# Causal attention layer with a sixth buffer of probabilities, its rotation tables loaded span by span

## The chip, the cores and the metric

The kernel runs on 1 core of one Trainium2 chip. The metric is the device time of one execution in microseconds (us), the median of several runs.

## The reference

One transformer layer in float32 on x of 4 batches, 2048 positions and 256 features, with 16 heads of 16. Attention with rotated queries and keys, then a block that projects onto cosines and sines of learned angles:

```python
qkv = layernorm(x) @ w_qkv                       # 256 -> 3 x 256
Q, K = Q * cos + rotate_half(Q) * sin, K * cos + rotate_half(K) * sin
attn = softmax(causal(Q @ K.T * 16 ** -0.5))     # per batch and head, 2048 x 2048
x = x + (attn @ V) @ w_proj + b_proj
real = layernorm(x) @ cos(theta + theta_noise)
imag = layernorm(x) @ sin(phi + phi_noise)
x = x + sqrt(real * real + imag * imag)
```

## The kernel before, in words

The work is cut into 16 units (u), each one batch and four heads, and each unit into four spans (c or t) of 512 positions, which makes 64 spans. A span has SUB (t + 1) steps of 128 keys against its 512 queries, 640 steps in all.

For each span (u, c), in this order:
- TensorE projects queries and keys (L1012), ScalarE copies them out as `raw` (L1158), SyncE's queue moves halves of it into `rot` (L742). GpSimd turns them (`rope`, L664 to L682: `raw` by `cos_t`, `rot` by `sin_t`, their sum, then three bf16 parts). SyncE lays the parts into `queries` and `stack_k` (L758). For the first two spans VectorE does the turning (L1360), and for the first five TensorE projects the swapped halves too (L1024).
- A first pass finds each query's maximum: TensorE multiplies queries by keys (L1057, items "max"), VectorE reduces the banks (L1399, L1394). GpSimd splits the negative maximum into three parts (L1510 and on), TensorE turns it (L1065, "turn"), VectorE copies it as `max_t` (L1351), SyncE lays it as three more rows of `queries` (L768).
- A second pass makes scores less the maximum (L1079), a step having four products of 512 columns, one a head, fewer columns on the diagonal. ScalarE takes the exponent (L1198) into `probs`, GpSimd zeroes the corner of diagonal tiles (L1526), and TensorE sums the values (L1094) into one bank that the whole span shares. ScalarE copies that bank out (L1205, "lift").
- Where four units of a batch are through, the rest of the layer runs for its blocks (L946, L935, L1001 and others).

Scores have four banks of the eight, the other work shares banks 2 to 6 with them, and the values' sum has the last. `probs` is a ring of `PROBS` buffers, one a step. Before it overwrites the buffer of step g, ScalarE waits until the values of step g - PROBS are summed:

```python
if g >= PROBS and n == 0:
    act.wait_ge(s_av, g - PROBS + 1)
```

Every engine follows a list, `ORDER[engine]`, in program order and waits on semaphores. The lists come from `plan()`, which runs before the kernel is built: every job has an engine, a duration, an aim in units of the whole (`at`), predecessors and a lag; engine by engine the job is taken that has the earliest aim among those that can start soon. The leads (`MAX_LEAD`, `QK_LEAD`, `EARLY`, `V_LEAD`, `X_LEAD`), `PATIENCE`, `SLACK`, `HOLD`, `RUN` and `STICK` are numbers of this planner and in no instruction. `TURN_COST` is its charge for a move between the values' products and all others, since the values' products stand side by side in the array (17 columns each, four at a time).

Names: `emptied` and `filled` are waits on a bank's reader and on its writer. `s_rope` counts seven operations of rotation a span. `PLACE[u, c]` is i, the number of a span in the order in which spans are projected.

Of the kernel before, what the change touches and what calls it, by code (L numbers as in the profile page):

```python
# [14 lines left out]
P = 128  # L15
BATCH, SEQ, DIM, HEADS = 4, 2048, 256, 16
# [5 lines left out]
KT = DIM // P  # L22
SPAN = 512
# [42 lines left out]
PROBS = 5  # L66
# [12 lines left out]
URGENT = .526  # L79
# [78 lines left out]
MAX_LEAD = .578  # L158
QK_LEAD = .737

EARLY = .545
X_LEAD = .189
V_LEAD = .418
SLACK = .9
PATIENCE = .008
# [5 lines left out]
TURN_COST = .1  # L171
MAX_FIRST = .033
HOLD = .763
STICK = 0
RUN = 4.358
TURN_LAG = .725
MAX_SLACK = .02
# [16 lines left out]
PACE = .924  # L194
LAST_AT = 15.4
LAST_PULL = .181
# [10 lines left out]
def plan():  # L207
# [41 lines left out]
    for c in range(1, SPANS):  # L249
        job(("tables", c), "SP", 0.9, CLOCK[0, c - 1] - 1.05, [("qk", 0, c - 1, KT - 1)], 5.0)  # L250
# [8 lines left out]
    for at, kind, u, c in sorted(todo):  # L259
# [12 lines left out]
        elif kind == "qk":  # L272
# [7 lines left out]
            free = [("rope", *last, ROPE_OPS - 1), *([("tables", c)] if c and u == 0 else [])] if i < ROPE_DVE else [used]  # L280
# [8 lines left out]
            for n in range(2 if i < ROPE_DVE else 0, ROPE_OPS):  # L289
                after = [("out", ("qk", u, c, 1)), ("rope", u, c, n - 1), ("rope", *last, ROPE_OPS - 1)]  # L290
                after += [("rot", u, c), ("out", ("qr", u, c))] if n in (1, 2) else []
                after += [("fetch", *ago), ("fetch_k", *ago)] if n == 3 else []
                after += [("tables", c)] if n == 0 and c and u == 0 else []
                if i < ROPE_DVE:
                    job(("rope", u, c, n), "DVE", 0.44 if n in (3, 5) else 0.69, at, after, 0.03 if n < ROPE_OPS - 1 else None)
                else:
                    job(("rope", u, c, n), "POOL", 0.7 if n in (3, 5) else 1.28, at, after)
# [191 lines left out]
def layer_kernel(nc, x, w_qk, w_v, w_proj, b_proj, theta, phi, theta_noise, phi_noise, cosines, sines,  # L489
# [7 lines left out]
    with ExitStack() as ctx:  # L497
# [44 lines left out]
        cos_t = sb("cos_t", [P, SEQ])  # L542
        sin_t = sb("sin_t", [P, SEQ])
# [49 lines left out]
        s_tables = [sem(f"rotation_tables_loaded{n}") for n in range(SPANS)]  # L593
# [58 lines left out]
        def rope(engine, ops, u, c, n):  # L652
            i = PLACE[u, c]
            span = slice(c * SPAN, (c + 1) * SPAN)
# [5 lines left out]
            if n == 0:  # L660
                emptied(engine, ("qk", u, c, 1))
                if i < FIRST * SPANS:
                    engine.wait_ge(s_tables[c], 32)
                ins = ops.tensor_tensor(turned[:, :], raw[:, i % 2, :], cos_t[:, span], ALU.mult)  # L664
            elif n == 1:
# [4 lines left out]
                ins = ops.tensor_tensor(crossed[:, :], rot[:, i % 2, :], sin_t[:, span], ALU.mult)  # L670
# [52 lines left out]
        with nc.Block() as block:  # L723
            @block.sync
            def _(sp):
# [142 lines left out]
                for name in ORDER["SP"]:  # L868
# [3 lines left out]
                    elif kind == "tables":  # L872
                        load_tables(name[1])
# [272 lines left out]
            def _(act):  # L1146
# [95 lines left out]
                act.dma_start(cos_t[:, 0:SPAN], cosines[:, 0:SPAN]).then_inc(s_tables[0], 16)  # L1242
                act.dma_start(sin_t[:, 0:SPAN], sines[:, 0:SPAN]).then_inc(s_tables[0], 16)
# [23 lines left out]
            def _(dve):  # L1267
# [75 lines left out]
                def reduce_out(item):  # L1343
# [9 lines left out]
                    if item[0] in ("qk", "qr"):  # L1353
                        u, c = item[1:3]
                        i, span = PLACE[u, c], slice(c * SPAN, (c + 1) * SPAN)
                        dve.wait_ge(s_tables[c], 32)
                        if i:
                            dve.wait_ge(s_rope, ROPE_OPS * i)
                        to, table = (turned, cos_t) if item[0] == "qk" else (crossed, sin_t)
                        nc.vector.tensor_tensor(to[:, :], bank, table[:, span], ALU.mult).then_inc(s_emptied["DVE"], 1)  # L1360
# [197 lines left out]
def tables():  # L1558
# [12 lines left out]
    return lay(cos), lay(sin), np.eye(P, dtype=np.float32), corner, one  # L1571
# [27 lines left out]
```

## Time and profile before

| | before |
|---|---|
| median of 3 runs | 1975.45 us (1974.7 to 1977.72) |
| profiled execution, its own time | 1979.04 us |
| span of its instructions | 1977.3 us |
| TensorE busy | 1939.0 us, 98% |
| VectorE / ScalarE / GpSimd busy | 1559.9 / 1389.1 / 871.0 us |
| bytes moved by DMA | 133.30 MB, 67 GB/s |
| matmul records | 12036 |

The span runs from the first to the last instruction of the profiled execution, and its own time has some 1.7 us around that. A matmul of float32 has several records. Matmuls overlap in their pipeline, so the distance between two starts tells what one costs, and a record's length does not.

### The profile page before, as it was taken

How to read it: one execution, taken by the hardware profiler on the slowest of the kernel's cores; microseconds unless marked ns; L12 is line 12 of the kernel's file. 1: busy time of each engine (PE TensorE's matmuls, PEld its weight loads, DVE VectorE, ACT ScalarE, POOL GpSimd, SP SyncE). 2: the span in 40 equal slices, each digit the busy share in tenths (PEclk: the TensorE clock that was granted, in tenths of full speed). 3: DMA queues.
4: the chain of work that ended last, by engine and by line, in shares of the span. 5: the costliest groups of instructions: out<-in, count | busy, mean ns of one | idle time of the engine just before them, and what ended most of it. 6: DMA issues, size and time to landing. Idle time of an engine off the chain costs nothing.

```text
span 1977.3 us, 38203 instructions
## 1 busy us (share of the span) xinstructions
PE 1939.0 (98%) x12036; PEld 798.1 (40%) x12036; DVE 1559.9 (79%) x4101; ACT 1389.1 (70%) x2687; POOL 871.0 (44%) x1336
## 2 busy tenths in 40 slices
PE   7999999999999999999999999999999999999998
PEld 4333433334443434343443443434444344433335
DVE  5898789988778787887877878888777877879725
ACT  3466668877676777877767777777767767777883
POOL 4714615443535454633544435553444545431232
PEclk9999999999999999999999999999999999999999
DMA  6301312122121221311222121322212212120131
GB/s 143 97 24 28 121 47 73 39 71 65 52 73 54 74 83 64 105 35 64 61 71 77 57 72 56 104 68 71 72 33 71 68 64 78 51 94 7 49 105 57
DMA packets 130762, 133.30 MB, mean 67 GB/s; under 512 B 29434, under 2 KB 105722, under 8 KB 130554
## 3 DMA queue, kind: packets, MB, share of 16 engines
q1 hardware_dynamic: 127728, 128.29, 21.1%
q10 hardware_dynamic: 2832, 2.56, 0.7%
q8 instruction: 97, 1.59, 0.3%
q14 instruction: 105, 0.86, 0.2%
HBM read 38.49 MB, written 25.68 MB: 32 GB/s over the span
## 4 chain that ended last, share of the span: by engine, by line
PE 87%; ACT 5%; issue 2%; DVE 2%; DMA 2%; POOL 1%; SPq 0%; DVEq 0%; POOLq 0%; ACTq 0%
PE banks L1094 23%; PE banks L1079 23%; PE banks L1057 22%; PE banks L1012 6%; PE banks L1001 6%; ACT probs L1198 3%; PE banks L1039 3%; PE banks L946 2%; DVE chunk_max L1399 1%; PE banks L935 1%; DMA squares<-sums 1%; PE banks L928 1%; PE banks L1065 0%; DVE banks L1394 0%; PE banks L1024 0%
## 5 line engine op out<-in xcount | busy, mean ns | idle before, releaser
L1198 ACT ACTIVATE probs<-banks 128x512 f32<-128x512 f32 (+1 forms) x2240 | 1143.9, 602 | 328.6 <-PE banks L1079 289.3
L1399 DVE TENSOR_REDUCE chunk_max<-banks 128x1 f32<-128x512 f32 x1536 | 985.3, 683 | 216.7 <-PE banks L1057 215.0
L1079 PE MATMUL banks<-queries,stack_k 99*128 99x512 bf16 (+3 forms) x2560 | 740.5, 350 | 11.8 <-ACT probs L1198 4.1
L1057 PE MATMUL banks<-stack_k,queries 96*128 96x512 bf16 (+3 forms) x2560 | 712.2, 349 | 8.2 <-DMA queries<-parts 2.8
L1394 DVE CUSTOM_DVE_ANT_0 banks<-banks,row_mask 128x128 f32<-128x128 f32 (+3 forms) x1024 | 483.7, 508 | 87.4 <-PE banks L1057 86.8
L1094 PE MATMUL banks<-probs,v_one 128*17 128x512 f32 (+3 forms) x5120 | 527.8, 532 | 1.1 <-POOL probs L1526 0.6
L1079 PEld LDWEIGHTS banks<-queries,stack_k 99*128 99x128 bf16 x2560 | 231.4, 97 | 435.9 <-ACT probs L1198 218.7
L1057 PEld LDWEIGHTS banks<-stack_k,queries 96*128 96x128 bf16 x2560 | 233.0, 97 | 310.9 <-DVE chunk_max L1399 67.3
L1526 POOL TENSOR_SCALAR_AFFINE_SELECT probs<-probs 128x512 f32<-128x512 f32 x256 | 160.9, 638 | 402.5 <-ACT probs L1198 402.0
L1094 PEld LDWEIGHTS banks<-probs,v_one 128*17 128x17 f32 x5120 | 119.7, 96 | 266.3 <-issue 173.7
L1394 DVE DVE_READ_ACCUMULATOR2_ANT chunk_max<- 128x1 f32 x1024 | 144.0, 141 | 0.0
L664 POOL TENSOR_TENSOR turned<-raw,cos_t 128x512 f32<-128x512 f32 x62 | 78.7, 1270 | 136.9 <-ACT raw L1158 135.4
L1012 PE MATMUL banks<-x_t,wqk 128*128 128x512 f32 x256 | 123.7, 606 | 0.7 <-ACT x_t L1153 0.5
L670 POOL TENSOR_TENSOR crossed<-rot,sin_t 128x512 f32<-128x512 f32 x62 | 80.8, 1304 | 61.3 <-DMA rot<-raw 58.3
L1510 POOL TENSOR_SCALAR max_neg<-row_max 128x16 f32<-128x16 f32 x64 | 19.2, 300 | 183.6 <-DVE row_max L1408 143.6
L1001 PE MATMUL banks<-wave,heads_t 128*128 128x512 f32 x208 | 98.7, 597 | 0.0
L1158 ACT ACTIVATE raw<-banks 128x512 f32<-128x512 f32 x62 | 37.4, 603 | 74.0 <-PE banks L1012 74.0
L672 POOL TENSOR_TENSOR turned<-turned,crossed 128x512 f32<-128x512 f32 x62 | 80.5, 1298 | 4.2
L1498 POOL TENSOR_TENSOR inverse<-squares 128x512 f32<-128x512 f32 x24 | 30.4, 1268 | 109.6 <-ACT squares L1177 109.6
L678 POOL TENSOR_TENSOR crossed<-turned,parts 128x512 f32<-128x512 f32 x62 | 71.8, 1158 | 4.6
L682 POOL TENSOR_TENSOR parts<-crossed,parts 128x512 bf16<-128x512 f32 x62 | 71.7, 1157 | 4.4
L1177 ACT ACTIVATE squares<-banks 128x512 f32<-128x512 f32 x52 | 31.1, 598 | 54.5 <-PE banks L1001 54.5
(158 smaller groups left out, 1162.3 us busy)
## 6 DMA issues: line engine op xcount, KB each, us to landing
queries<-parts SPq DMA_DIRECT2D x384, 64.0 KB, 2.6
stack_k<-parts SPq DMA_DIRECT2D x354, 64.0 KB, 2.6
sums<-o_raw SPq DMA_DIRECT2D x64, 256.0 KB, 2.3
rot<-raw SPq DMA_DIRECT2D x236, 64.0 KB, 2.0
xin<-x SPq DMA_DIRECT2D x17, 512.0 KB, 4.2
mid<-x SPq DMA_DIRECT2D x13, 512.0 KB, 5.1
heads_t<-sums SPq DMA_DIRECT2D x26, 256.0 KB
inverse<-inverses SPq DMA_DIRECT2D x26, 256.0 KB
```

The costliest lines, as they stand in the source:

```text
L664: ins = ops.tensor_tensor(turned[:, :], raw[:, i % 2, :], cos_t[:, span], ALU.mult)
L670: ins = ops.tensor_tensor(crossed[:, :], rot[:, i % 2, :], sin_t[:, span], ALU.mult)
L672: ins = ops.tensor_tensor(turned[:, :], turned[:, :], crossed[:, :], ALU.add)
L1001: mm = nc.tensor.matmul(bank, turned3[finish_set(n)][:, k, j * P:(j + 1) * P], wave[:, k, :], start=(k == 0), stop=(k == KT - 1))
L1012: mm = nc.tensor.matmul(psum[BANK[item]], wqk[:, u % GROUPS, k, :], x_t[:, k, c * SPAN:(c + 1) * SPAN], start=(k == 0), stop=(k == KT - 1) ...
L1057: mm = nc.tensor.matmul(bank[:, n * wide:(n + 1) * wide], queries[0:SPLIT_ROWS, query_place(u, t), h + n, j * P:(j + 1) * P], stack_k[u % ...
L1079: mm = nc.tensor.matmul(bank[:, a * wide:(a + 1) * wide], stack_k[u % 2][0:ROWS, j // SUB, first + a, (j % SUB) * P:(j % SUB + 1) * P], qu ...
L1094: mm = nc.tensor.matmul(out_bank[VW * h:VW * h + VC, w0:SPAN], v_one[u // 2 % 2][:, j, HG * (u % 2) + h, :], probs[:, g % PROBS, h, w0:SPA ...
L1198: nc.scalar.activation(probs[:, g % PROBS, first:first + many, w0:SPAN], bank, ACT.Exp).then_inc(s_exp, 1)
L1394: ins = nc.vector.tensor_tensor_reduce(out=scores_of, in0=scores_of, in1=row_mask[:, SPAN - wide:SPAN], scale=1.0, scalar=LOWEST, op0=ALU. ...
L1399: nc.vector.tensor_reduce(to, bank[:, 0:count * wide].rearrange("p (h n) -> p h n", h=count), AX.X, ALU.max).then_inc(s_emptied["DVE"], 1)
L1526: nc.gpsimd.affine_select(out=square, in_=square, compare_op=ALU.is_ge, fill=0.0, base=0, pattern=[[0, HG], [1, P]], channel_multiplier=-1 ...
```

## The change

Three things. The tables `cos_t` and `sin_t`, 8 KB each in every partition and loaded once, go. In their place stands `turn_t`, two buffers of 4 KB that hold cosines and sines of one span. It is loaded for each of the 64 spans with one DMA of 512 KB (ScalarE's queue has the first, SyncE's the other 63), and a load waits until the span two before has read its buffer. The 8 KB that come free are a sixth buffer of `probs`. And the planner's numbers are others, among them those below, so all lists are made anew (`SLACK` .9 to 1.3, `PATIENCE` .008 to .012, `HOLD` .763 to .542, `RUN` 4.358 to 4.842, `STICK` 0 to .001, `V_LEAD` .418 to .325, `PACE` .924 to .989 besides).

```diff
-PROBS = 5
+PROBS = 6
...
-MAX_LEAD = .578
-QK_LEAD = .737
-EARLY = .545
+MAX_LEAD = 0.63
+QK_LEAD = 0.718
+EARLY = 0.691
...
-    for c in range(1, SPANS):
-        job(("tables", c), "SP", 0.9, CLOCK[0, c - 1] - 1.05, [("qk", 0, c - 1, KT - 1)], 5.0)
...
+            if i:
+                job(("tables", u, c), "SP", 0.6, at - 0.1, [("qk", *last, KT - 1), *([used] if i > 1 else [])], 4.0)
+            free = [("rope", *last, ROPE_OPS - 1), ("tables", u, c)] if i < ROPE_DVE else [used]
...
-                after += [("tables", c)] if n == 0 and c and u == 0 else []
+                after += [("tables", u, c)] if n == 0 else []
...
-        cos_t = sb("cos_t", [P, SEQ])
-        sin_t = sb("sin_t", [P, SEQ])
+        turn_t = sb("turn_t", [P, 2, 2, SPAN])
...
             if n == 0:
                 emptied(engine, ("qk", u, c, 1))
-                if i < FIRST * SPANS:
-                    engine.wait_ge(s_tables[c], 32)
-                ins = ops.tensor_tensor(turned[:, :], raw[:, i % 2, :], cos_t[:, span], ALU.mult)
+                engine.wait_ge(s_tables[i % 2], 16 * (i // 2 + 1))
+                ins = ops.tensor_tensor(turned[:, :], raw[:, i % 2, :], turn_t[:, i % 2, 0, :], ALU.mult)
...
-                ins = ops.tensor_tensor(crossed[:, :], rot[:, i % 2, :], sin_t[:, span], ALU.mult)
+                ins = ops.tensor_tensor(crossed[:, :], rot[:, i % 2, :], turn_t[:, i % 2, 1, :], ALU.mult)
...
-                def load_tables(c):
-                    columns = slice(c * SPAN, (c + 1) * SPAN)
-                    sp.dma_start(cos_t[:, columns], cosines[:, columns]).then_inc(s_tables[c], 16)
-                    sp.dma_start(sin_t[:, columns], sines[:, columns]).then_inc(s_tables[c], 16)
+                def load_tables(u, c):
+                    i = PLACE[u, c]
+                    if i - 2 in range(ROPE_DVE):
+                        emptied(sp, ("qr", *PROJECTED[i - 2]))
+                    elif i >= 2:
+                        sp.wait_ge(s_rope, ROPE_OPS * (i - 2) + 2)
+                    sp.dma_start(turn_t[:, i % 2, :, :], rotations[:, c, :, :]).then_inc(s_tables[i % 2], 16)
...
-                act.dma_start(cos_t[:, 0:SPAN], cosines[:, 0:SPAN]).then_inc(s_tables[0], 16)
-                act.dma_start(sin_t[:, 0:SPAN], sines[:, 0:SPAN]).then_inc(s_tables[0], 16)
+                act.dma_start(turn_t[:, 0, :, :], rotations[:, 0, :, :]).then_inc(s_tables[0], 16)
...
-    return lay(cos), lay(sin), np.eye(P, dtype=np.float32), corner, one
+    return np.stack([lay(cos), lay(sin)], 1).reshape(P, 2, SPANS, SPAN).transpose(0, 2, 1, 3), np.eye(P, dtype=np.float32), corner, one
```

In the lists below the lines of the changed kernel are mostly one higher (L1095 is L1094). All instructions of computation are the same in kind and number, but for one filler product.

TensorE, unit 2, its first span of four diagonal steps (the values of 512, 384, 256 and 128 columns). Before, from the second of these steps to the third; L1057 is a product for a maximum, L1079 one for scores:

```order
L1094 MATMUL banks<-probs,v_one 17x384 x4
L1057 MATMUL banks<-stack_k,queries 128x512 x2
L1057 MATMUL banks<-stack_k,queries 128x128 x4
L1079 MATMUL banks<-queries,stack_k 128x128 x4
L1057 MATMUL banks<-stack_k,queries 128x512
L1079 MATMUL banks<-queries,stack_k 128x512
L1057 MATMUL banks<-stack_k,queries 128x512 x2
L1079 MATMUL banks<-queries,stack_k 128x512 x2
L1057 MATMUL banks<-stack_k,queries 128x512
L1079 MATMUL banks<-queries,stack_k 128x512
L1094 MATMUL banks<-probs,v_one 17x256 x4
```

The changed kernel, from the end of the same span's scores on:

```order
L1058 MATMUL banks<-stack_k,queries 128x512
L1058 MATMUL banks<-stack_k,queries 128x256 x2
L1095 MATMUL banks<-probs,v_one 17x512 x4
L1095 MATMUL banks<-probs,v_one 17x384 x4
L1095 MATMUL banks<-probs,v_one 17x256 x4
L1095 MATMUL banks<-probs,v_one 17x128 x4
L1080 MATMUL banks<-queries,stack_k 128x512 x2
L1058 MATMUL banks<-stack_k,queries 128x512 x2
```

The four steps of values, which stood in four places, now stand in one.

TensorE, the start: from the turn of the first span's maxima (L1065) to its first scores. Before:

```order
L1065 MATMUL banks<-ident_bf,max_parts 48x128
L1057 MATMUL banks<-stack_k,queries 128x512 x2
L1057 MATMUL banks<-stack_k,queries 128x128 x4
L1057 MATMUL banks<-stack_k,queries 128x512 x2
L1057 MATMUL banks<-stack_k,queries 128x256 x2
L1057 MATMUL banks<-stack_k,queries 128x512 x2
L1039 MATMUL banks<-wv,x_t 128x128 x8
L1057 MATMUL banks<-stack_k,queries 128x256 x2
L1057 MATMUL banks<-stack_k,queries 128x512
L1057 MATMUL banks<-stack_k,queries 128x384
L1079 MATMUL banks<-queries,stack_k 128x512
```

The changed kernel (L1066, L1058 and L1080 are the same lines):

```order
L1066 MATMUL banks<-ident_bf,max_parts 48x128
L1058 MATMUL banks<-stack_k,queries 128x512 x2
L1058 MATMUL banks<-stack_k,queries 128x128 x4
L1058 MATMUL banks<-stack_k,queries 128x512 x2
L1058 MATMUL banks<-stack_k,queries 128x256 x2
L1058 MATMUL banks<-stack_k,queries 128x512 x2
L1058 MATMUL banks<-stack_k,queries 128x256 x2
L1058 MATMUL banks<-stack_k,queries 128x512
L1058 MATMUL banks<-stack_k,queries 128x384
L1080 MATMUL banks<-queries,stack_k 128x512 x2
```

The projection of values (L1039) has left this stretch, and the first scores come two at a time. It stands now behind the projections of unit 1's first two spans.

SyncE's queue, about a third of the way, where a block's last part is under way. Before:

```order
L742 DMA rot<-raw 32x512 x4
L768 DMA queries<-max_t 1x16x128 x3
L848 DMA mid<-x 128x4x256
L774 DMA sums<-o_raw 128x512
L768 DMA queries<-max_t 1x16x128 x3
L742 DMA rot<-raw 32x512 x4
L758 DMA queries<-parts 16x4x512 x6
L758 DMA stack_k<-parts 16x4x512 x6
L768 DMA queries<-max_t 1x16x128 x3
```

The changed kernel, the same stretch:

```order
L735 DMA turn_t<-rotations 128x1024
L743 DMA rot<-raw 32x512 x4
L775 DMA sums<-o_raw 128x512
L769 DMA queries<-max_t 1x16x128 x3
L735 DMA turn_t<-rotations 128x1024
L743 DMA rot<-raw 32x512 x4
L735 DMA turn_t<-rotations 128x1024
L743 DMA rot<-raw 32x512 x4
L769 DMA queries<-max_t 1x16x128 x3
```

A table load stands ahead of each move of halves. All through the program 34 of SyncE's 63 loads have such a move directly behind them, and six have the rows of a maximum (L769).

## Rows read from the trace of the kernel before

**Rows 1.** The page, parts 1 and 2: engines, and the granted TensorE clock in 40 slices.

```profile
PE 1939.0 (98%) x12036; PEld 798.1 (40%) x12036; DVE 1559.9 (79%) x4101; ACT 1389.1 (70%) x2687; POOL 871.0 (44%) x1336
...
PEclk9999999999999999999999999999999999999999
```

**Rows 2.** The page, part 4: the chain that ended last, by engine and by line.

```profile
PE 87%; ACT 5%; issue 2%; DVE 2%; DMA 2%; POOL 1%; SPq 0%; DVEq 0%; POOLq 0%; ACTq 0%
PE banks L1094 23%; PE banks L1079 23%; PE banks L1057 22%; PE banks L1012 6%; PE banks L1001 6%; ACT probs L1198 3%; PE banks L1039 3%; PE banks L946 2%; DVE chunk_max L1399 1%; PE banks L935 1%; DMA squares<-sums 1%; PE banks L928 1%; PE banks L1065 0%; DVE banks L1394 0%; PE banks L1024 0%
```

**Rows 3.** Windows of all engines: busy us (instructions), clock, DMA share, GB/s.

```profile
0.00:100.00 100.00, 83.76 (x462) 38.72 (x463) 70.50 (x206) 37.22 (x68) 60.44 (x103) 0.97 0.50 119
...
1300.00:1700.00 400.00, 398.90 (x2491) 164.72 (x2489) 318.97 (x832) 288.76 (x561) 188.39 (x260) 1.00 0.22 66
...
1884.00:1896.00 12.00, 11.95 (x76) 2.74 (x68) 1.78 (x2) 12.00 (x27) 3.31 (x2) 1.00 0.27 94
```

**Rows 4.** Waits: engine, line, releaser: us in total, times, longest.

```profile
ACT probs L1198 <- PE banks L1079: 289.3, 220, 3.6
PEld banks L1079 <- ACT probs L1198: 218.7, 609, 1.0
...
ACT probs L1198 <- PE banks L1094: 29.4, 23, 2.2
```

**Rows 5.** Timeline of TensorE at 403 us: start, us, instructions.

```profile
402.96 0.38 PE L1057 MATMUL banks<-stack_k,queries 96*128 96x512 bf16 x1
403.18 0.38 PE L1079 MATMUL banks<-queries,stack_k 99*128 99x512 bf16 x1
403.40 0.38 PE L1057 MATMUL banks<-stack_k,queries 96*128 96x512 bf16 x1
403.62 0.38 PE L1079 MATMUL banks<-queries,stack_k 99*128 99x512 bf16 x1
403.93 1.91 PE L1094 MATMUL banks<-probs,v_one 128*17 128x512 f32 x16
405.77 0.39 PE L1079 MATMUL banks<-queries,stack_k 99*128 99x512 bf16 x1
```

**Rows 6.** Timeline of TensorE in the last unit, where no maxima are left, 1885 us.

```profile
1884.51 1.04 PE L1079 MATMUL banks<-queries,stack_k 99*128 99x512 bf16 x4
1885.48 1.05 PE L1094 MATMUL banks<-probs,v_one 128*17 128x512 f32 x8
1886.46 1.05 PE L1079 MATMUL banks<-queries,stack_k 99*128 99x512 bf16 x4
```

**Rows 7.** Timeline of all engines around the first scores.

```profile
44.46 0.24 PE L1065 MATMUL banks<-ident_bf,max_parts 128*48 128x128 bf16 x1
...
46.06 1.86 SPq L768 DMA_DIRECT2D queries<-max_t  x3
...
48.77 2.02 PE L1039 MATMUL banks<-wv,x_t 128*128 128x128 f32 x16 [0.35 <-DVE chunk_max L1399]
...
51.96 0.38 PE L1079 MATMUL banks<-queries,stack_k 99*128 99x512 bf16 x1 [0.57 <-DMA queries<-max_t]
```

**Rows 8.** Timeline of the start: a table load, and the rotation that reads it.

```profile
24.44 1.58 SPq L733 DMA_DIRECT2D cos_t<-cosines  x1
...
34.83 1.28 POOL L664 TENSOR_TENSOR turned<-raw,cos_t 128x512 f32<-128x512 f32 x1 [4.28 <-ACT raw L1158]
```

**Rows 9.** Tile cos_t, then tile max_t: duration min/median/max; landings min/median/max.

```profile
L733 SPq DMA_DIRECT2D cos_t<-cosines x3: 506/611/1577, 12.9 to 30.0; - x3
...
DMA to landing us min/median/max: 4.0/5.1/6.1
...
L768 SPq DMA_DIRECT2D queries<-max_t x192: 502/589/1623, 46.1 to 1879.4; - x192
...
DMA to landing us min/median/max: 1.6/1.7/4.5
```

**Rows 10.** The page, part 3: the hardware DMA queue of SyncE.

```profile
q1 hardware_dynamic: 127728, 128.29, 21.1%
```

More of the change, by code:

```diff
@@ L78 @@
 ROPE_DVE = 2
-URGENT = .526
+URGENT = 0.526
 HELP = 5
@@ L157 @@
 MASKED_HEADS = 4
-MAX_LEAD = .578
-QK_LEAD = .737
-EARLY = .545
[L162 to L165, printed above, removed]
+MAX_LEAD = 0.63
+QK_LEAD = 0.718
+EARLY = 0.691
+X_LEAD = 0.187
+V_LEAD = 0.325
+SLACK = 1.3
+PATIENCE = 0.012
 TRIG_AT = 2.0
@@ L170 @@
 OTHER_BANKS = range(2, 7)
[L171 to L177, printed above, removed]
+TURN_COST = 0.1
+MAX_FIRST = 0.036
+HOLD = 0.542
+STICK = 0.001
+RUN = 4.842
+TURN_LAG = 0.76
+MAX_SLACK = 0.02
 FINISHED = [SPANS * b + t for b in range(BATCH) for u, t in SCORED if u == GROUPS * b + GROUPS - 1]
@@ L192 @@
 IN_HALVES = range(BLOCKS - SPANS, BLOCKS)
-PACE = .924
+PACE = 0.989
 LAST_AT = 15.4
-LAST_PULL = .181
+LAST_PULL = 0.181
 SETS = SPANS
@@ L279, in plan @@
                 before_qk = ("qk", u, c, k)
-            free = [("rope", *last, ROPE_OPS - 1), *([("tables", c)] if c and u == 0 else [])] if i < ROPE_DVE else [used]
+            if i:
+                job(("tables", u, c), "SP", 0.6, at - 0.1, [("qk", *last, KT - 1), *([used] if i > 1 else [])], 4.0)
+            free = [("rope", *last, ROPE_OPS - 1), ("tables", u, c)] if i < ROPE_DVE else [used]
             reader, took = ("DVE", 0.69) if i < ROPE_DVE else ("ACT", 0.6 if i < HELP else 0.5)
@@ L486, with layer_kernel @@
     NUMBER |= {item: n for n, item in enumerate(name for name in ORDER["PE"] if READER.get(name) == _e)}
-def layer_kernel(nc, x, w_qk, w_v, w_proj, b_proj, theta, phi, theta_noise, phi_noise, cosines, sines,
+def layer_kernel(nc, x, w_qk, w_v, w_proj, b_proj, theta, phi, theta_noise, phi_noise, rotations,
                  identity, corner, ones, w_last, sums, inverses, out):
@@ L592, in layer_kernel @@
         s_wv = sem("value_weights_loaded")
-        s_tables = [sem(f"rotation_tables_loaded{n}") for n in range(SPANS)]
+        s_tables = [sem(f"rotation_tables_loaded{n}") for n in range(2)]
         s_corner = sem("diagonal_mask_loaded")
@@ L653, in rope @@
             i = PLACE[u, c]
-            span = slice(c * SPAN, (c + 1) * SPAN)
             if i < ROPE_DVE and n == 2:
@@ L872, in _ @@
                     elif kind == "tables":
-                        load_tables(name[1])
+                        load_tables(*name[1:])
                     elif kind == "wv":
@@ L1354, in reduce_out @@
                         u, c = item[1:3]
-                        i, span = PLACE[u, c], slice(c * SPAN, (c + 1) * SPAN)
-                        dve.wait_ge(s_tables[c], 32)
+                        i = PLACE[u, c]
+                        dve.wait_ge(s_tables[i % 2], 16 * (i // 2 + 1))
                         if i:
                             dve.wait_ge(s_rope, ROPE_OPS * i)
-                        to, table = (turned, cos_t) if item[0] == "qk" else (crossed, sin_t)
-                        nc.vector.tensor_tensor(to[:, :], bank, table[:, span], ALU.mult).then_inc(s_emptied["DVE"], 1)
+                        to, table = (turned, 0) if item[0] == "qk" else (crossed, 1)
+                        nc.vector.tensor_tensor(to[:, :], bank, turn_t[:, i % 2, table, :], ALU.mult).then_inc(s_emptied["DVE"], 1)
                         return
@@ L1577 @@
     from concourse.bass_utils import run_bass_kernel_spmd
-    cosines, sines, eye, corner, one = tables()
+    rotations, eye, corner, one = tables()
     w = np.asarray(L0_attn_w_qkv)
@@ L1587 @@
         "theta": L0_ffn_theta, "phi": L0_ffn_phi, "theta_noise": L0_ffn_theta_noise, "phi_noise": L0_ffn_phi_noise,
-        "cosines": cosines, "sines": sines, "eye": eye, "corner": corner, "one": one,
+        "rotations": rotations, "eye": eye, "corner": corner, "one": one,
         "w_last": w_last.reshape(P, DIM),
```

## The prediction

> **What bounds the kernel now.** I read the page from the top: engines first, then the chain, then the windows, the waits, and last the timeline of TensorE.
>
> TensorE is busy 98% of the span, at full clock in every slice [rows 1], and the chain that ended last lies on it for 87%, with ScalarE 5%, VectorE 2% and DMA 2% [rows 2]. All the products remain, so the change can only save time between them. The windows say where such time is: in the first 100 us TensorE is busy 83.76, from 1300 to 1700 us 398.90 of 400 [rows 3]. The page's busy time flatters it, though, since matmuls overlap. The distance between two starts is the honest measure, and rows 5 show it: products of 512 columns start 0.22 us apart, so each sets its own pace, but before the values' products (L1094) the distance is 0.31.
>
> So there are two kinds of lost time. One is the move between the values' products, of 17 columns side by side, and the rest, of 128 columns. Going in costs 0.31 - 0.22 = 0.09 us. For the way out: one step of values takes 0.98 us to the next start [rows 6], two steps take 1.84 [rows 5], so a step is 0.86 and what is left over is 0.12, some of it rounding. I take 0.10 us a change. The other kind is waiting for a bank: the weight loads of scores stand idle 218.7 us for ScalarE in 609 waits, short ones that the pipeline mostly covers [rows 4]. On the chain the exponents (L1198) hold 3%, 59 us, and the maxima's reduction (L1399) 1% [rows 2]. ScalarE in turn waits 289.3 us for scores and only 29.4 us, in 23 waits, for values [rows 4]. The latter holds what five buffers of `probs` cost, together with the bank of the values' sum, for which the same row stands. So the ring is rarely the limit by itself. What a sixth buffer buys is freedom for the order: values may wait longer and go in fewer, longer stretches.
>
> **Changes between kinds of product.** I counted them in the two lists of TensorE. The values stand in 302 stretches before and in 281 now, 21 fewer, thus 42 changes fewer. The turns of maxima, of 48 columns, are a kind of their own: 27 of their edges touched a stretch of values, now 15, which costs 12 changes back. In all 715 become 685, and 30 x 0.10 = 3.0 us is saved. TensorE pays them itself, one behind the other, so this is on the path except where ScalarE is the limit. It is that in the last unit, busy 12.00 of 12 us [rows 3]; there the change is free and saves nothing, but few of the 30 lie there.
>
> A page of the Trainium skill bears on this price: TensorEngine Tiling (Array Packing), section Key Properties, says that changing the tiling mode, not just the tile, drains the TensorE. By that rule longer stretches are always better. The trace agrees at 0.09 us on the way in; against it stands that a longer stretch keeps scores from ScalarE, which the rule does not price.
>
> **Waits at the banks.** No row prices one stretch's waits. The lower bound is nothing: the same exponents follow the same scores. The upper is the chain's 59 us on L1198 shared among 302 stretches, 0.20 us each, for 21 stretches 4.1 us. I take the upper one, as the sixth buffer loosens the 23 waits for values besides, and keep 0 for the range. Beyond it, half of the 29.4 us, 14.7, is the most that I can imagine from a ring that no longer binds; it is a rival below.
>
> **The start.** Between the turn of the first maxima at 44.46 us and the first scores at 51.96 lie 7.5 us [rows 7]. The order has only some 3.4 us of products there, at rows 5's pace; the rest is waiting for VectorE and, at the end, 0.57 us for the three DMAs of rows [rows 7]. In this hole the projection of values (2.02 us, 48.77) cost next to nothing. It is moved out, and must be paid later in full if TensorE has no hole there: between 0 and 2.0 us lost, I take 1.0. Scores that come two at a time win a little of it back.
>
> **Table loads.** SyncE issues 63 loads in place of six DMAs, ScalarE one in place of two. An issue takes 0.61 us at the median and lands 5.1 us later (4.0 to 6.1) for 256 KB [rows 9]; these are of 512 KB. That is 63 x 0.61 = 38 us of issue on a queue that has the whole span for it, less 4 us. The bytes: 64 loads of 0.52 MB less 2.1 MB for the old tables are 31.5 MB more, on 128.29 MB that held 21.1% of the engines [rows 10], so some 5% more, in bursts. A load's own wait, on the second rotation step of the span two before, is the one that the move of halves already had. Where the load stands directly ahead of that move (34 places), GpSimd starts the rotation not with `raw` but up to 6 us later. It is cover that pays: in the order the maxima that need a span begin 60 us or more of products behind its projection, in both kernels, from unit 1 on. Only unit 0 is tight, with 8 to 42 us. Its third span's table was issued at 24.44 us and read at 34.83 [rows 8]; now its issue waits for the same queue place, and 24.44 + 1.58 + 6.1 = 32.1 is still before 34.83. With that cover gone, each late microsecond would be one of the start. I set the loads at 0.
>
> **The rest.** The leads of the maxima grow (`MAX_LEAD`). From turn to first scores of a span the order has at least 10.8 us of products before and 17.7 now, from unit 1 on, against 7.5 that the transfer needed at its slowest [rows 7]: late rows become less likely, which cost little already. The price stands at the end, where 92 products of scores are left behind the last maximum instead of 87, in the stretch that ScalarE limits: five times the difference of an exponent (some 0.49 us, 12.00 us over some 24.5) and a product (0.22), 1.4 us at most, and the finish products lie between. I set 0.
>
> **Sum.** -3.0 - 4.1 + 1.0 = -6.1 us. Against the profiled execution's own 1979.04 that is 1972.9. It lies 3.6 us above the median of the three runs, 1975.45, so for the median the sum gives 1969.3 us. A measurement of this kernel can tell about 0.2%, 4 us, from no change.
>
> **Rivals.**
> (a) Only the counted changes come: the waits at the banks move elsewhere, since ScalarE's work is the same and a stretch of three full values steps, 0.86 x 3 = 2.6 us, outlasts four full banks of 0.6. Stretches of three full steps' columns or more grow from 47 to 53. Then -3.0 + 1.0 = -2.0, 1973.5 us. For it: VectorE is at 80% and ScalarE at 72% from 1300 to 1700 us, where TensorE hardly waits [rows 3]; there is little to win there. Chance 0.27.
> (b) The ring was the limit: 14.7 us of ScalarE's waits for values come back, -3.0 - 14.7 + 1.0, 1958.8 us. Against it: 23 waits of 640 steps [rows 4]. Chance 0.13.
> (c) Slower: rows of a maximum land behind a table in unit 0. The DMAs are busy half of the first 100 us [rows 3], rows landed after 1.7 us at the median and after 4.5 at worst [rows 9], and the order, counted at the pace of rows 5, leaves 2.5, 4.4, 5.6 and 9.0 us of products between turn and scores in the four spans of unit 0. If three of them wait the table's 6.1 us less the 1.7, 3 x 4.4 = 13.2, the sum is -6.1 + 13.2 = +7.1, 1982.5 us. It decides from two late spans on. Against it: behind unit 0 the lead is 17.7 us, and TensorE has VectorE to wait for at the start anyway. Chance 0.12.
> The Trainium skill, DMA: Bandwidth & Descriptors, section Queues, rings and completion order, says that a DMA's semaphore lands only after every earlier write of the same DMA engine, across queues. By that rule (c) would strike wherever rows follow a table within some 6 us; no row here shows the two together.
> (d) That the sixth buffer isn't used: the order excludes it, since the values of 54 steps stand behind scores five or six steps ahead, and before those of 25.
>
> **How the numbers follow.** The forecast, 1969.3, has 0.48, the rivals 0.27, 0.13 and 0.12. The range reaches from just above (b), as its full price is an extreme, to a little over the end of (a) with 2.0 lost at the start and a late span: 1959.5 to 1978.5. Faster by over 0.2% is below 1971.5: all of (b) and most of the forecast's 0.48, in which the waits may give only part, and a little of (a), 0.61 together. Slower is above 1979.4: 0.11 of (c) and 0.01 for the rest, 0.12. Within lies 0.27.
>
> **What would show it.** Right: TensorE's busy time nearly the same and the span shorter by 4 to 9 us; ScalarE's waits for values below 29.4 us in 23; the chain's share on L1198 a little below 3%; turn_t landing in 4 to 8 us, and GpSimd waiting for it ahead of a rotation with nobody waiting behind. Wrong: the first 100 us busier or emptier by more than 2 us than 83.76, TensorE waiting for `queries<-max_t` or `queries<-parts` after unit 0, or ScalarE's waits for scores above 289.3 us with the chain's ScalarE share above 5%, which would be starvation by the longer stretches.

## The result and the profile after

The changed kernel took 1984.77 us (median of 5 runs, 1977.54 to 1990.46) against 1976.64 for the kernel before on the same chip: ratio 1.0042, interval 1.0024 to 1.0061. It is slower, by about 8 us, where the prediction's sum was 6.1 us of gain, its forecast 1969.3 us and the top of its range 1978.5. A second series, of 12 runs, gave 1984.2 us and 1.0032 (1.0019 to 1.0046), so the sign stands.

The page of the changed kernel: TensorE's row, the granted clock in 40 slices, SyncE's queue, and the two lines on the chain that ended last.

```profile
PE 1948.0 (98%) x12034; PEld 805.0 (40%) x12034; DVE 1559.4 (78%) x4101; ACT 1388.9 (70%) x2687; POOL 870.5 (44%) x1336
...
PEclk9989999899999999999999999999999999999999
...
q1 hardware_dynamic: 135936, 159.75, 26.5%
...
PE 85%; ACT 4%; DMA 3%; SPq 3%; issue 2%; DVE 1%; POOL 1%; ACTq 0%; DVEq 0%; POOLq 0%
PE banks L1080 23%; PE banks L1095 22%; PE banks L1058 22%; PE banks L1002 5%; PE banks L1013 5%; PE banks L1040 3%; ACT probs L1199 3%; PE banks L947 2%; SPq L759 1%; DMA rot<-raw 1%; SPq L743 1%; PE banks L936 1%; PE banks L929 1%; PE banks L1066 1%; DMA xin<-x 0%
```

Against [rows 1, 2] three things are to be seen. TensorE's share is still 98%, but its clock is below 90% in two slices, the third (99 to 149 us) and the eighth (348 to 398 us). The chain now holds SyncE's queue with 3% and DMAs with 3%, among them the move of halves (`rot<-raw`), which stood nowhere in it. And the queue moves 159.75 MB for 128.29 [rows 10], as computed.

Where did the time go? The share of busy time cannot say, since TensorE's busy time grows when its clock falls. I took the distances between the starts of its products, as the prediction did at rows 5, over the whole profiled execution, and split them into three: the pace of the products themselves, 0.097 us for each change of kind (fitted over the traces; the prediction's rows gave 0.09 on the way in and 0.12 on the way out), and what is left, which is waiting and lost clock. The first two are a fit, so their split from the third is an estimate.

| us, TensorE from first to last product | before | after | difference |
|---|---|---|---|
| the products' own pace | 1809.1 | 1808.5 | -0.6 |
| changes of kind | 69.4 (715) | 66.4 (685) | -3.0 |
| lost | 86.3 | 102.1 | +15.8 |
| of it 0 to 100 us | 21.3 | 23.3 | +2.0 |
| of it 100 to 200 us | 5.4 | 12.5 | +7.1 |
| of it 200 to 500 us | 10.1 | 21.1 | +11.0 |
| of it 500 to 1900 us | 39.6 | 34.3 | -5.3 |
| of it the rest | 6.3 | 7.6 | +1.3 |

(The parts count waits of at least 20 ns, so they add up to a little less.) The sum, +12.2, stands for the two profiled executions, 1979.04 and 1990.46 us; the medians differ by 8.1. The changed kernel's profiled execution was the slowest of its five. So in this pair a gain like the forecast one is there, in the changes and in the body of the program, and some 20 us of losses in the first 500 us eat it up. Two places hold most of them. A second profile of the same kernel (1983.11 us, near its median) has the losses from 100 to 200 us and from 300 to 400 us again, each within 1 us, but not the one in the first 100 us: there it lost less than the kernel before. And at 1337 us it has no wait of that length.

**Place A, 341 to 372 us.** Timeline of the changed kernel, all engines (start, duration, instructions, idle time before with what ended it):

```profile
340.87 1.06 SPq L775 DMA_DIRECT2D sums<-o_raw  x2
...
341.97 0.45 SPq L735 DMA_DIRECT2D turn_t<-rotations  x1
342.46 1.20 SPq L727 DMA_DIRECT2D xin<-x  x2
...
343.71 0.50 SPq L735 DMA_DIRECT2D turn_t<-rotations  x1
344.31 2.67 SPq L743 DMA_DIRECT2D rot<-raw  x4
...
346.66 1.28 POOL L662 TENSOR_TENSOR turned<-raw,turn_t 128x512 f32<-128x512 f32 x1 [1.09 <-DMA turn_t<-rotations]
...
354.08 1.27 POOL L668 TENSOR_TENSOR crossed<-rot,turn_t 128x512 f32<-128x512 f32 x1 [6.14 <-DMA rot<-raw]
...
358.42 2.07 ACT L1212 ACTIVATE xin<-xin,shift,rstd 128x256 f32<-128x256 f32 x4 [5.40 <-POOL shift L698]
...
361.03 1.91 PE L1095 MATMUL banks<-probs,v_one 128*17 128x512 f32 x8 [3.95 <-ACT probs L1199]
```

Read it from the bottom. TensorE waits 3.95 us for exponents. ScalarE had not made them because it stood 5.40 us at the normalisation of the next block's `x` (L1212), which is ahead of them in its list. That waits for GpSimd's shift (L698), and GpSimd stood 6.14 us at the rotation's second half, for `rot<-raw`. The four transfers of `rot` were issued behind two sums, two tables and two pieces of `x`, 2.5 MB in 3.4 us. They usually land after 2.3 us. Here the last of the four, which sets GpSimd free, landed after 7.7, the longest of all 236. The rotation itself was in no hurry: its span's maxima come much later, as the prediction said. What was in a hurry stood behind it, on two engines' in-order lists.

Then comes a second price. Windows of the changed kernel (PE, PEld, DVE, ACT and POOL busy, each with its count; granted clock, DMA share, GB/s):

```profile
345.00:360.00 15.00, 11.90 (x82) 4.18 (x80) 13.28 (x50) 7.65 (x16) 7.12 (x13) 0.98 0.81 235
360.00:372.00 12.00, 10.97 (x45) 2.72 (x46) 4.79 (x15) 7.36 (x15) 9.18 (x19) 0.60 0.10 24
```

For 15 us the DMA engines are 81% busy and TensorE is idle 3.1 us. In the next 12 us it waits one more and does 45 products only: from 359.3 us on, while it still waited, it was granted 1.2 GHz in place of 2.4, for 10.2 us. The same happens, smaller, at two more places. A product that starts at 480.07 us has waited 2.90 us, and the clock is halved for 6.8 us from 478.8 on. The one at 1337.45 has waited 2.36 us for GpSimd's `max_parts`, which stand there behind another wait for `rot<-raw`, of 3.74 us; the clock is halved for 3.4 us from 1338.9 on. The first of these, in the same kind of timeline:

```profile
478.66 1.23 DVE L1309 TENSOR_TENSOR heads_t<-heads_t,inverse 128x1024 f32<-128x1024 f32 x1 [5.43 <-DMA inverse<-inverses]
479.81 0.21 DVE L1351 COPY max_t<-banks 48x128 bf16<-48x128 bf16 x1
480.07 0.61 PE L1058 MATMUL banks<-stack_k,queries 96*128 96x512 bf16 x1 [2.90 <-DVE max_t L1351]
```

Again the late transfer (`inverse`, issued at 470.08 us) isn't what TensorE needs. It needs the small copy of 0.21 us that stands behind the transfer's reader on VectorE. That the table loads made this transfer late is argued from the run with the move first, below, and not shown in this trace.

In all the changed kernel has some 41 us at half clock, in stretches of 3.4, 6.8 and 10.2 us; the kernel before has some 10.

**Place B, 100 to 120 us.** Windows of the kernel before, then of the changed one:

```profile
100.00:110.00 10.00, 9.91 (x81) 4.84 (x80) 9.66 (x27) 5.41 (x11) 3.54 (x5) 1.00 0.15 48
110.00:120.00 10.00, 9.75 (x54) 2.67 (x52) 10.00 (x23) 6.79 (x13) 0.00 (x0) 1.00 0.18 61
```

```profile
100.00:110.00 10.00, 8.86 (x65) 2.87 (x63) 10.00 (x26) 3.89 (x8) 4.49 (x10) 1.00 0.17 57
110.00:120.00 10.00, 9.62 (x23) 2.91 (x23) 10.00 (x24) 3.30 (x6) 0.00 (x0) 0.51 0.17 58
```

VectorE is full in both. In the changed kernel TensorE has little else than maxima here, and each waits for it:

```profile
109.20 0.39 PE L1058 MATMUL banks<-stack_k,queries 96*128 96x256 bf16 x2 [0.21 <-DVE chunk_max L1399]
109.80 0.39 PE L1058 MATMUL banks<-stack_k,queries 96*128 96x512 bf16 x1 [0.21 <-DVE chunk_max L1399]
...
119.40 2.41 PE L1040 MATMUL banks<-wv,x_t 128*128 128x128 f32 x16
```

The projection of values, which filled this stretch at 107.61 us before, now stands at 119.40. From 110 us on the clock is halved for 10.2 us, and 23 products run where 54 did.

### The profile page after: what moved, and what is told of

It reads as the page before. It is cut to its first block, busy times and chain, and to the rows that moved or that the text cites. A ratio compares the mean times of both kernels' runs of the same rounds, so it can differ in the third digit from the quotient of the medians.

```text
span 1988.7 us, 38254 instructions
## 1 busy us (share of the span) xinstructions
PE 1948.0 (98%) x12034; PEld 805.0 (40%) x12034; DVE 1559.4 (78%) x4101; ACT 1388.9 (70%) x2687; POOL 870.5 (44%) x1336
## 3 DMA queue, kind: packets, MB, share of 16 engines
q1 hardware_dynamic: 135936, 159.75, 26.5%
## 4 chain that ended last, share of the span: by engine, by line
PE 85%; ACT 4%; DMA 3%; SPq 3%; issue 2%; DVE 1%; POOL 1%; ACTq 0%; DVEq 0%; POOLq 0%
PE banks L1080 23%; PE banks L1095 22%; PE banks L1058 22%; PE banks L1002 5%; PE banks L1013 5%; PE banks L1040 3%; ACT probs L1199 3%; PE banks L947 2%; SPq L759 1%; DMA rot<-raw 1%; SPq L743 1%; PE banks L936 1%; PE banks L929 1%; PE banks L1066 1%; DMA xin<-x 0%
## 5 line engine op out<-in xcount | busy, mean ns | idle before, releaser
L1199 ACT ACTIVATE probs<-banks 128x512 f32<-128x512 f32 (+1 forms) x2240 | 1139.9, 600 | 340.8 <-PE banks L1080 314.3
L1080 PE MATMUL banks<-queries,stack_k 99*128 99x512 bf16 (+3 forms) x2560 | 737.5, 351 | 5.8 <-ACT probs L1199 1.9
L1058 PE MATMUL banks<-stack_k,queries 96*128 96x512 bf16 (+3 forms) x2560 | 716.4, 351 | 12.0 <-DMA queries<-parts 2.9
L1095 PE MATMUL banks<-probs,v_one 128*17 128x512 f32 (+3 forms) x5120 | 524.3, 532 | 4.3 <-ACT probs L1199 4.3
L1080 PEld LDWEIGHTS banks<-queries,stack_k 99*128 99x128 bf16 x2560 | 234.3, 97 | 416.4 <-ACT probs L1199 219.6
L1058 PEld LDWEIGHTS banks<-stack_k,queries 96*128 96x128 bf16 x2560 | 233.9, 98 | 338.3 <-DVE chunk_max L1399 80.3
L1095 PEld LDWEIGHTS banks<-probs,v_one 128*17 128x17 f32 x5120 | 121.3, 97 | 270.1 <-issue 168.3
L668 POOL TENSOR_TENSOR crossed<-rot,turn_t 128x512 f32<-128x512 f32 x62 | 80.5, 1299 | 58.3 <-DMA rot<-raw 54.3
L662 POOL TENSOR_TENSOR turned<-raw,turn_t 128x512 f32<-128x512 f32 x62 | 78.9, 1272 | 40.4 <-issue 30.4
L1206 ACT ACTIVATE o_raw<-banks 128x512 f32<-128x512 f32 x64 | 38.6, 603 | 44.1 <-PE banks L1095 43.8
```

Source lines behind the costliest of these rows:

```text
L662: ins = ops.tensor_tensor(turned[:, :], raw[:, i % 2, :], turn_t[:, i % 2, 0, :], ALU.mult)
L668: ins = ops.tensor_tensor(crossed[:, :], rot[:, i % 2, :], turn_t[:, i % 2, 1, :], ALU.mult)
L1058: mm = nc.tensor.matmul(bank[:, n * wide:(n + 1) * wide], queries[0:SPLIT_ROWS, query_place(u, t), h + n, j * P:(j + 1) * P], stack_k[u % ...
L1080: mm = nc.tensor.matmul(bank[:, a * wide:(a + 1) * wide], stack_k[u % 2][0:ROWS, j // SUB, first + a, (j % SUB) * P:(j % SUB + 1) * P], qu ...
L1095: mm = nc.tensor.matmul(out_bank[VW * h:VW * h + VC, w0:SPAN], v_one[u // 2 % 2][:, j, HG * (u % 2) + h, :], probs[:, g % PROBS, h, w0:SPA ...
L1199: nc.scalar.activation(probs[:, g % PROBS, first:first + many, w0:SPAN], bank, ACT.Exp).then_inc(s_exp, 1)
```

## The experiments

Three questions: is it the table loads or the plan of the work; within the loads, is it their bytes or their place in the queue; and what do the sixth buffer and the numbers do apart from each other. Kernels that ran together shared a chip and its runs of the kernel before.

**Tables of almost no bytes.** The rows that are left out keep the angles of earlier spans; lists and waits are those of the changed kernel.

```diff
+rows = slice(0, P if i < 8 else 4)
-sp.dma_start(turn_t[:, i % 2, :, :], rotations[:, c, :, :])
+sp.dma_start(turn_t[rows, i % 2, :, :], rotations[rows, c, :, :])
```

> The changed kernel, whose table loads from the ninth span on carry 4 partitions instead of 128 (the other rows of the tables stay those of earlier spans, so later rotations use wrong angles): same orders, same waits, same number of issues, 29 MB less traffic. Theory T1 (the bytes of the table loads crowd other transfers, which land late, in-order engines stand behind them, and TensorE's clock then falls to half): 1966 to 1973 us, granted clock back at about 0.997, no landing of rot over 4.5 us. Theory T2 (the new orders themselves leave the waits, the bytes are harmless): 1982 to 1988 us, clock 0.989 to 0.993 as before.

1971.3 us, ratio 0.9969 (0.9957 to 0.9982). Without the bytes, the change as a whole is faster than the kernel before. Two of the signs were missed: the granted clock came back to 0.993 to 0.995 only (the stretch at half clock from 109 us on is still there), and the longest landing of `rot` was 5.1 us.

**All bytes, but another place in the queue.** Wherever a table load stood directly ahead of a move of halves (34 places), the two change places in SyncE's list. Nothing else differs.

```diff
+for _n in range(len(ORDER["SP"]) - 1):
+    _a, _b = ORDER["SP"][_n:_n + 2]
+    if _a[0] == "tables" and _b[0] == "rot":
+        ORDER["SP"][_n:_n + 2] = [_b, _a]
```

> The changed kernel with one edit of SyncE's list: wherever a table load stands directly ahead of a move of halves, the two change places, so the move no longer stands behind 512 KB. T1 with the table itself as the obstacle (T3: the place in the queue decides): most of the loss comes back, 1972 to 1978 us, median landing of rot 2.0 us again. T1 with crowding by several large transfers together: little changes, 1981 to 1987 us, since x blocks and other loads still stand ahead. T2: 1982 to 1988 us.

1973.17 us, 0.9979 (0.9970 to 0.9989). Timeline of this kernel at place A:

```profile
342.32 2.57 SPq L747 DMA_DIRECT2D rot<-raw  x4
...
344.93 0.58 SPq L739 DMA_DIRECT2D turn_t<-rotations  x1
...
349.13 1.27 POOL L672 TENSOR_TENSOR crossed<-rot,turn_t 128x512 f32<-128x512 f32 x1 [3.15 <-DMA rot<-raw]
```

And its windows:

```profile
345.00:360.00 15.00, 14.49 (x104) 4.87 (x96) 14.51 (x56) 11.13 (x22) 10.67 (x21) 1.00 0.58 170
360.00:372.00 12.00, 11.96 (x75) 4.17 (x75) 10.57 (x35) 10.46 (x21) 10.54 (x20) 1.00 0.20 58
```

The rotation runs 5 us earlier (2 of them this kernel was already ahead at its last rotation, 329.61 for 331.66 us), TensorE has no wait of over 1.5 us behind it, it does 104 and 75 products in place of 82 and 45, and the clock stays full. Over the whole profiled execution 83.3 us are lost in place of 102.1; of these 18.8 us, 16.6 lie in the three hundreds of us from 300, from 400 and from 1300 on, where the long waits stood. As many bytes, the same numbers, the same buffers: the queue place alone is worth the 10 us. VectorE's wait for `inverse` also fell, from 5.43 to 2.85 us, and TensorE's wait of 2.90 us behind it is gone.

**Half the bytes.** The rows of the first experiment with `P // 2` in place of 4.

> The changed kernel whose table loads from the ninth span on carry 64 partitions instead of 128 (the other rows stay those of earlier spans, so later rotations use wrong angles there). T1 says that the loss grows with the bytes ahead of other transfers: between 1971.3 us (4 partitions) and 1984.8 us (128), 1974 to 1980 us. If any large load ahead does the harm whatever its size: 1982 to 1988 us.

1984.63 us, 1.0030 (1.0015 to 1.0045): nothing gained. Timeline of this kernel at place A, and its windows:

```profile
351.80 1.27 POOL L668 TENSOR_TENSOR crossed<-rot,turn_t 128x512 f32<-128x512 f32 x1 [5.28 <-DMA rot<-raw]
```

```profile
345.00:360.00 15.00, 12.52 (x89) 4.22 (x87) 13.09 (x49) 9.63 (x19) 8.85 (x17) 0.97 0.64 157
360.00:372.00 12.00, 12.00 (x69) 3.99 (x65) 9.00 (x30) 9.18 (x19) 10.13 (x23) 0.89 0.11 25
```

The forecast of 1974 to 1980 us, a loss that grows with the bytes, was missed. GpSimd's wait is graded: 6.14 us with full tables, 5.28 with half, 3.37 with four rows, 3.15 with the move first. The cost isn't: at 5.28 us TensorE still waits 2.48 us in this stretch, at 3.37 and 3.15 it has no such wait. Some 3 to 5 us, by an estimate from these four, is what stood as slack between the rotation and the engines behind it. The kernel still lost 3.4 us of half clock at 359 us, and as much again at 854 and 1329.

**The ring alone taken back.** The changed kernel with five buffers.

```diff
-PROBS = 6
+PROBS = 5
```

> The changed kernel with five buffers of probabilities, planned anew with the same numbers; table loads as in the changed kernel. T1: as slow as the changed kernel, 1983 to 1990 us, clock 0.989 to 0.994. If the sixth buffer's longer stretches are the cause (part of T2): back to 1975 to 1979 us.

1998.71 us, 1.0102 (1.0082 to 1.0122), slower than either theory had it. **The ring and the tables without the numbers:** the changed code planned with the numbers of before.

> The changed kernel with the planner's numbers of the kernel before (six buffers, tables span by span). Changes between kinds of product 711, stretches of values 302, as before. T1: slow, 1980 to 1990 us, clock under 0.995, since the table loads are all there. T2 with the numbers as the cause: 1974 to 1978 us.

1987.34 us, 1.0054 (1.0038 to 1.0069). The time is the one that the theory of the bytes had forecast, but its cause is another: the clock is at 0.995 to 0.998, not under 0.995, and the run of this plan with the move first, below, gains nothing. The profiled execution took 7.4 us more than that of before, 1986.39 for 1979.04: 2.9 for more filler products (products that the plan puts where it expects TensorE to have nothing else), 4.3 for more waits (90.6 us for 86.3), and 0.4 less for changes, 711 of them. Here is where the fillers stand, in TensorE's timeline near the end, for the kernel before and for this one:

```profile
1939.69 1.95 PE L1102 MATMUL banks<-ident 128*128 128x128 f32 x16
```

```profile
1942.58 6.41 PE L1103 MATMUL banks<-ident 128*128 128x128 f32 x56
```

**Tables span by span, and nothing else:** five buffers, numbers of before.

> The kernel before with the tables loaded span by span and nothing else: five buffers, the planner's numbers of before, planned anew since the load is a job of SyncE's list. It prices the table loads alone. T1 (bytes ahead of other transfers make in-order engines wait): 1983 to 1995 us. If the loads cost nothing on this order, 1975 to 1979 us.

1976.96 us beside 1975.94, 1.0010 (0.9998 to 1.0022). **The numbers and nothing else:** the kernel before, five buffers and whole tables, with the changed numbers.

> The kernel before with the changed kernel's planner numbers and nothing else: whole tables, five buffers. With the ring of five these numbers make 745 changes between kinds of product and 311 stretches of values, more than before. If the numbers serve only with six buffers: 1980 to 1992 us; if they are good by themselves: under 1975 us.

1998.71 us, 1.0113 (1.0095 to 1.0131), again slower than forecast. It has the stretch at half clock too, 10.2 us from 108 us on, with neither ring nor table loads. **The ring and the tables again,** with the numbers of before, and the move of halves put first.

> The run with six buffers, loads span by span and the numbers of before (1987.3 us), with the move of halves put ahead of the table load wherever they stood side by side. If the place in the queue is the cause in general: 1974 to 1981 us. If what helped the changed kernel was peculiar to its order: 1984 to 1990 us.

1988.65 us, 1.0067 (1.0053 to 1.0082). Moving the halves first, worth 10 us in the changed kernel, is worth nothing here. In this plan the DMA engines are quiet where the other has its jam. Windows of the kernel with ring and tables and the numbers of before, tables first:

```profile
345.00:360.00 15.00, 14.40 (x95) 5.22 (x88) 14.06 (x57) 12.23 (x25) 4.62 (x18) 1.00 0.02 4
```

The parts side by side:

| buffers | tables | numbers | move | ratio to before | changes | lost us, profiled |
|---|---|---|---|---|---|---|
| 5 | whole | before | | 1 | 715 | 86.3 |
| 5 | by span | before | after table | 1.0010 | 714 | 83.1 |
| 6 | by span | before | after table | 1.0054 | 711 | 90.6 |
| 6 | by span | before | first | 1.0067 | 711 | 94.5 |
| 5 | whole | after | | 1.0113 | 745 | 102.9 |
| 5 | by span | after | after table | 1.0102 | 729 | 105.9 |
| 6 | by span | after | after table | 1.0042 | 685 | 102.1 |
| 6 | by span | after | first | 0.9979 | 685 | 83.3 |

The effects don't add. The loads by themselves cost nothing that can be measured, which was the forecast, with five buffers and either set of numbers (1 to 1.0010, 1.0113 to 1.0102); each time the lists were planned anew. Only in the changed kernel's own plan do they cost, 10 us by their place in the queue. The sixth buffer by itself costs 0.4% with the numbers of before (1.0010 to 1.0054) and gains 0.6% (1.0102 to 1.0042) with the others. The 30 fewer changes belong to the pair: with five buffers the new numbers make 729 of them, with six the old numbers 711.

**Place B.** First `EARLY`, back to .545, on top of the move put first:

> The changed kernel with the move of halves first (1973.2 us), and EARLY back at 0.545, so that the first units' projections come later. Theory T4: from 100 to 120 us TensorE waits for VectorE and then runs at half clock for 10.2 us, some 6 us more lost than before in that stretch, since more projections and maxima are drawn ahead. If EARLY does it: 1965 to 1970 us and no half clock at 110 us. If MAX_LEAD does: 1971 to 1975 us, half clock there as before.

1974.53 us, 0.9990 (0.9979 to 1.0001). The stretch at half clock from 108 us on is still there; missed. Then the lead of one projection of values:

```diff
-todo.append((first - V_LEAD, "v", u // 2, c))
+todo.append((first - (.45 if (u, c) == (0, 3) else V_LEAD), "v", u // 2, c))
```

> The changed kernel with the move of halves ahead of the table load (1973.2 us), and one aim of the planner changed: the values of unit 0's last span are projected earlier (lead 0.45 instead of 0.325), so that this float32 work stands again between the maxima at 105 to 113 us, as in the kernel before. The last 5243 of TensorE's 5609 jobs are the same. Theory T5: in that stretch only maxima are left, TensorE waits 0.2 us for VectorE ahead of each, and the half clock of 10.2 us follows. Then no half clock at 110 us and 1966 to 1970 us. If VectorE is simply the limit there: the half clock may go but the time stays at 1971 to 1975 us.

1973.15 us, 0.9974 (0.9966 to 0.9983), beside 1974.23 for the same kernel without it: missed as well, as 1.1 us is too little to be told from none here. Windows of this kernel:

```profile
100.00:110.00 10.00, 9.96 (x79) 4.64 (x78) 10.00 (x25) 3.87 (x8) 3.88 (x9) 1.00 0.18 59
110.00:120.00 10.00, 8.41 (x24) 2.12 (x27) 9.97 (x24) 3.54 (x6) 0.00 (x0) 0.70 0.15 51
```

The first ten microseconds are mended, 79 products in place of 65. The hole has moved into the next ten, with 24 products, and the half clock with it, to 114 us (6.8 us long). So the projection's place decides where TensorE runs dry, not whether. The stretch has too few products beside the maxima, for which VectorE sets the pace. Which number would bring some in, as the plan of before had them, stays open.

**Two again, on one chip:** the changed kernel, and the same with the move of halves first.

> The changed kernel itself once more, to compare with the others on one chip. The times of its five runs lay between 1977.5 and 1990.5 us with clocks of 0.993 to 0.989. All theories expect 1982 to 1988 us at the median, and again the slowest runs at the lowest clock.

> The changed kernel with the move of halves ahead of the table load once more, on the same chip as the changed kernel: 1971 to 1975 us if the place in the queue is the cause, and no further than 0.2% from the changed kernel if the first comparison was chance.

1984.2 us (1.0032) and 1974.23 us (0.9983, 0.9974 to 0.9991). Side by side on one chip the difference is 10.0 us, and 10.3 between their profiled executions (1983.11 and 1972.86). By the distances of TensorE's starts, some 6.6 us of it lie between 300 and 400 us: place A holds two thirds. GpSimd's wait there was 6.31 us with the table first and 3.25 with the move first. Four of the stretches of half clock came back at the same places, at 50, 108, 358 and 477 us with the table first (the last for 3.4 us this time), and at 47 and 108 with the move first; the one at 1339 us did not.

## Why the prediction was wrong

**Changes of kind: right.** 715 became 685 in the trace, and at the fitted 0.097 us this is 3.0 us, as forecast. The experiments add what the prediction didn't know, that neither the ring nor the numbers does it alone.

**Waits at the banks: right in kind, too small.** I took 4.1 us. From 500 to 1900 us the lost time fell by 5.3 in the changed kernel and by 8.2 with the move first (39.6 to 31.4). That it was the ring's doing, as I argued, is not shown: ring and numbers brought it together, and each of them alone was slower. ScalarE's waits for values went from 29.4 us in 23 to 17.7 in 15. Waits of the changed kernel:

```profile
ACT probs L1199 <- PE banks L1080: 314.3, 258, 8.4
...
ACT probs L1199 <- PE banks L1095: 17.7, 15, 2.3
```

The waits for scores grew, from 289.3 to 314.3, which I had named as a sign of starvation by longer stretches. It is not one: the chain's ScalarE share fell, from 5% to 4%, and with the move first these waits are 306.5 and the kernel is the faster.

**The start: the term was mis-sized.** I took 1.0 us for the projection of values that leaves the first hole, asking only whether it must be paid where it goes. From 100 to 200 us the changed kernel lost 7.1 us more than before. (The 2.0 us more in the first 100 us stand in one profiled execution and not in the other.) What I left out is what stands where the projections used to be: maxima alone, at VectorE's pace, and the clock that falls behind them. That the loss belongs to the numbers is shown by the ring of five with the same numbers (12.7 us lost from 100 to 200 us) and by the numbers alone, which lose as much there, against some 5.4 in the kernels with the numbers of before. That moving the projection accounts for it is not shown; the experiment on its lead speaks against it.

**The table loads: the step that failed.** "It is cover that pays: in the order the maxima that need a span begin 60 us or more of products behind its projection, in both kernels, from unit 1 on." The traces bear that out: TensorE waited for `queries<-parts` once in the changed kernel, 2.9 us in unit 0, as before (2.8). And the loads by themselves did cost nothing in the old plan. But in this one, where I set them at 0, their place ahead of the move of halves cost 10.0 us. I asked only who reads the rotated span. I had the right number in hand, that GpSimd starts the rotation up to 6 us late, and did not ask what is queued behind it: GpSimd's deviations for the next block, and behind those ScalarE's normalisation and then its exponents. The wait was 6.14 us, the slack of those neighbours between 3.15 and 5.28, estimated from those two runs.

**The clock: a term that was missing.** In this kernel each stall of 2 to 4 us came with 3.4 to 10.2 us at half clock. That about doubled the price of each: at place A the 3.95 us wait and the slices around it cost about 9 us in the changed kernel against 2 with the move first (lost from 300 to 400 us: 9.6 and 1.7).

Rival (c) had the sign but not the place. It looked for rows of a maximum late behind a table in unit 0; TensorE waited 1.5 us for such rows once, for 0.6 before, and that was all. It named the right cause, a small transfer behind a big one in a queue. The Trainium skill, DMA: Bandwidth & Descriptors, section Queues, rings and completion order, was quoted there for a semaphore that lands only after earlier writes of the same engine. The 64 KB move that landed after 7.7 us, with 2.5 MB issued ahead of it and its three fellows, agrees with it. A shared rate would do too, by an estimate: 235 GB/s at a share of 0.81 is 290 GB/s for engines that are full, and 2.5 MB take 8.6 us at that. No run here tells the two apart.

So the sum by the measured terms, for the profiled executions: -3.0 for changes, -5.3 for waits in the body, +9.1 for the first 200 us, +11.0 for the jams from 200 to 500 us, +1.3 at the end and -0.6 in the products' own pace, together 12.5 where 12.2 was counted. With the move first the profiled executions differ by -5.9, but that one of before was 3.6 us above its median. The medians give -4.3 and -3.3 us on two chips: a gain of the forecast sign, of some half to two thirds of its size, with the stretch from 108 us on still unmended.

## What to carry to other kernels

Before a load of many bytes is put into a queue of small transfers, look for each small one directly behind it, and ask for its reader not only who needs the result, but what else stands behind the reader on its own engine, and behind that on the next. If they may be exchanged, put the small one first; here that exchange was worth 0.5%. A freed resource and the plan that uses it are one change: here each half alone was slower than the kernel before, and the two together, with the move first, were faster by 0.2%. Either experiment alone would have condemned them.

## What the hardware showed that was not expected

A stall of TensorE can cost more than itself. With waits of 3.95, 2.90 and 2.36 us in an engine otherwise full came 10.2, 6.8 and 3.4 us at a granted clock of one half. In the first two the clock fell while TensorE waited, in the third 1.5 us after. A series of waits of only 0.21 us each between maxima came ahead of 10.2 us. It isn't so each time: in the ring of five a wait of 2.65 us at 1098 us passed at full clock, and in the kernel with the numbers alone one of 2.58 at 836. Over the five runs of the changed kernel the time goes with the clock, from 1977.54 us at a mean of 0.993 to 1990.46 at 0.989. That the clock's answer to the stalls makes part of the scatter is likely, and not shown.

And transfers of 64 KB, 2.0 us at the median before (4.3 at most), took up to 7.7 us behind 2.5 MB. With the tables cut to four rows the longest was 5.1, with the move first 6.2: other big loads still stood near them in the queue, `x` and the sums among them.
